# 52 of 72 attention probability tiles are turned in 32x32 blocks by VectorE, and their value products run in 32x64 tiles of TensorE

## The chip, the cores and the metric

One core of a Trainium2 chip runs the whole kernel in one launch. The metric is the device time of that launch in microseconds (us), the median of several runs.

## The reference

Two layers on 4 sequences of 1024 tokens with 256 channels, all in float32. The first layer (a linear attention with a running sum, then a mixture of 16 experts) and the last part (a mixture of 8 experts with a gate) are not touched. The change is in the attention of the second layer:

```
q, k, v = (rows of the normalized x) @ Wq, Wk, Wv      # 16 heads of 64 columns
q, k = apply_rope(q), apply_rope(k)                     # t * cos + rotate_half(t) * sin
sim = (q * 64 ** -0.5) @ k.T, masked above the diagonal
out = softmax(sim) @ v                                  # per head, 1024 x 64
y = concat(out) @ Wo
```

The two heads of a pair are computed together, so there are 8 pairs for each of 4 sequences.

## The kernel before, in words

The function `attention` is called twice: once for three sequences ("at", with the routing of the following mixture of experts beside it) and, after the mixture of experts, once for the last sequence ("at2", with the gating of the finished sequences on GpSimd). Each call runs 8 pairs a sequence, one turn of the loop a pair. What each engine does in a turn, and in which order, is written out in strings: `PE_ORDER`, `ACT_ORDER`, `DVE_ORDER` (lines 1192 to 1197) for TensorE, ScalarE and VectorE. A word is a kind of step with its numbers; a plus sign means that the step belongs to the next pair, so that two pairs overlap. `PE_FIRST`, `ACT_FIRST` and `DVE_FIRST` are the fill. The steps, with t the block of 128 query rows (0 to 7), k the block of 128 key rows and e the head of the pair:

- **A** (TensorE, lines 1550 and 1556): projections. For each half of 512 tokens, A0/A4 is q, A1/A5 is k (two products of 512 columns each), A2, A3, A6, A7 are v, 256 tokens each. ScalarE copies q and k to `raw` (line 1634), VectorE copies v (line 1843).
- **swap** (SyncE's queue, line 1383): four copies within SBUF exchange the halves of each head into `swapped`. **P** (VectorE, line 1850): raw x cos and swapped x sin. **rotate** (GpSimd, line 1656) adds the two into `qkT`.
- **S** (TensorE, line 1565): scores of row block t, chunk c of up to 512 keys. The two heads lie in rows 0 to 63 and 64 to 127 of the array. **M** (VectorE, line 1830) adds the mask, writes the piece to `p` and keeps the row's negated maximum. **E** (ScalarE, line 1621) is the exponential in place, with the row sum.
- **T** (TensorE, line 1573): the probability tiles of 128x128, 36 a head, 72 a pair, are transposed into PSUM, up to four a bank, and ScalarE copies them to `pT` (line 1628, 20 copies a turn).
- **V** (TensorE, line 1587): values times `pT`, for 256 queries at a time (V0 to V3); the two heads use columns 0 to 63 and 64 to 127 of the array. ScalarE copies the result to `oT` (line 1640). **W** (TensorE, line 1597) is the output product; VectorE adds it, divided by the row sum, to `y` (line 1865; the reciprocals are **I**, line 1837).

The eight banks of PSUM are used in a ring, in the order of TensorE's string: the step that uses a bank again waits until it is read (`free`, line 1507). `p` has eight buffers (`LAG`), two per row block. On SyncE's queue stand the loads of the next weights, the swaps and, in "at2", the loads and stores of the gating (`pair`, line 1385). GpSimd adds in "at" the rows that it scatters to the experts (`send`), and in "at2" `begin`, `plus` and `finish` of the gating (lines 1673 to 1692); the tanh of the gating is ScalarE's, in front of the step named by `CLOSE_TANH`.

## Time and profile before

| | |
|---|---|
| median of 3 runs | 2525.26 us (2525.19 to 2533.8) |
| the profiled execution | 2526.91 us |
| its span, first to last instruction | 2525.0 us |
| mean granted clock of TensorE | 0.985 of full speed |
| a turn of the pair loop, in both stages | 39.35 us |
| the "at2" stage | 2182 to 2525 us of the span, 8 turns |

A busy share is the part of the span in which the engine works on something; TensorE's weight loads are listed apart from its matmuls and overlap them. A float32 matmul shows as two records, a transpose as one, and a matmul's record is longer than the distance to the next, because consecutive ones overlap in the array. So steps are read from start to start.

### The profile page before, as it was taken

To read this page: it belongs to the slowest core of one execution; us is meant where nothing else is said; L and a number is where in the kernel's file an instruction comes from. 1 tells how busy PE (TensorE), PEld (TensorE's weight loads), DVE (VectorE), ACT (ScalarE), POOL (GpSimd) and SP (SyncE) were. 2 spreads that over 40 slices of the span, in tenths; PEclk is the share of its full clock that TensorE was granted. 3 is DMA by queue.
4 is the path that set the end of the run, shared out by engine and by line. 5 is a ranking of instruction groups with operands and counts; after the bars stand their busy time and mean duration, and the time that the engine had idled before them with its cause. 6 is when DMAs were issued, how large, how long until landed. Compare 5 with 4: busy or idle time off the path is not lost. (4 is left out here: it accounts for less than half of the span.)

```text
span 2525.0 us, 45013 instructions
## 1 busy us (share of the span) xinstructions
PE 2423.9 (96%) x14680; PEld 1710.0 (68%) x14681; DVE 1316.0 (52%) x3690; ACT 1105.4 (44%) x2581; POOL 606.9 (24%) x535
## 2 busy tenths in 40 slices
PE   7999999999986999999999999998999999799997
PEld 5555555666665566666666666666899999566665
DVE  6766242222246766666666666665333333366665
ACT  3211111111124566666666666666222222276665
POOL 4002002444454233332111111110111111224341
PEclk9999999999989999999999999999999999899999
DMA  6013104965456132332111222122777676324331
GB/s 214 17 50 117 50 17 135 268 210 156 109 146 212 51 99 78 109 100 68 40 35 42 58 68 57 44 58 78 253 239 241 236 244 233 109 76 126 90 96 59
DMA packets 133964, 296.04 MB, mean 117 GB/s; under 512 B 16865, under 2 KB 87025, under 8 KB 123473
## 3 DMA queue, kind: packets, MB, share of 16 engines
q1 hardware_dynamic: 112896, 251.59, 31.4%
q0 software_dynamic: 20944, 42.94, 6.6%
q8 instruction: 60, 0.98, 0.2%
q14 instruction: 64, 0.52, 0.1%
HBM read 193.80 MB, written 67.12 MB: 103 GB/s over the span
## 5 line engine op out<-in xcount | busy, mean ns | idle before, releaser
L1621 ACT ACTIVATE at_p<-at_p,at_nmax 128x640 f32<-128x640 f32 (+7 forms) x512 | 392.5, 767 | 185.9 <-DVE at_nmax L1830 184.3
L1656 POOL TENSOR_TENSOR kept_big<-kept_xg 128x1024 f32<-128x1024 f32 x64 | 151.0, 2359 | 896.3 <-DVE kept_xg L1850 896.3
L1628 ACT ACTIVATE at_pT<-at_ps 128x512 f32<-128x512 f32 (+1 forms) x640 | 311.3, 573 | 106.6 <-PE at_ps L1573 106.6
L1830 DVE CUSTOM_DVE_ANT_0 at_p<-at_ps,atk_mask 128x512 f32<-128x512 f32 (+3 forms) x512 | 281.9, 585 | 141.9 <-PE at_ps L1565 141.2
L1573 PEld LDWEIGHTS at_ps<-kept_ident,at_p 128*128 128x128 f32 x2304 | 257.9, 142 | 111.3 <-issue 60.3
L1573 PE MATMUL at_ps<-kept_ident,at_p 128*128 128x128 f32 x2304 | 304.8, 278 | 11.5 <-ACT at_p L1621 10.8
L1565 PE MATMUL at_ps<-kept_big 64*128 64x512 f32 (+3 forms) x1536 | 299.9, 509 | 15.3 <-POOL kept_big L1656 12.5
L1587 PE MATMUL at_ps<-at_pT,at_v 128*64 128x256 f32 (+1 forms) x2560 | 270.2, 362 | 2.5 <-issue 2.5
L1865 DVE SCALAR_TENSOR_TENSOR kept_big<-at_ps,at_inv,kept_big 128x256 f32<-128x256 f32 x512 | 214.2, 476 | 88.2 <-issue 67.1
L1587 PEld LDWEIGHTS at_ps<-at_pT,at_v 128*64 128x64 f32 x2560 | 174.0, 137 | 115.7 <-issue 29.0
L1550 PE MATMUL at_ps<-atk_h,atk_w 128*128 128x512 f32 x512 | 239.9, 603 | 12.5 <-SPq L1364 12.5
L1065 PE MATMUL ex_ps<-kept_big 128*128 128x512 f32 x480 | 210.2, 597 | 0.9 <-ACT kept_big L1122 0.9
L1969 PEld LDWEIGHTS moe_ps<-moe_xT,moe_w 128*128 128x128 f32 x1696 | 197.6, 192 | 3.6 <-ACT moe_xT L2002 0.9
L1969 PE MATMUL moe_ps<-moe_xT,moe_w 128*128 128x128 f32 x1696 | 198.0, 275 | 0.7 <-ACT moe_xT L2002 0.7
L1565 PEld LDWEIGHTS at_ps<-kept_big 64*128 64x128 f32 x1536 | 129.2, 190 | 88.8 <-issue 53.5
L1065 PEld LDWEIGHTS ex_ps<-kept_big 128*128 128x128 f32 x480 | 91.9, 192 | 110.4 <-issue 109.7
L1127 ACT ACTIVATE kept_big<-ex_ps 128x512 f32<-128x512 f32 x64 | 38.2, 597 | 290.4 <-PE ex_ps L1065 268.3
L1947 POOL DMA_INDIRECT z_rows<-late_yo,late_to x71 | 68.8, 969 | 371.9 <-DVE late_yo L2030 371.9
L1550 PEld LDWEIGHTS at_ps<-atk_h,atk_w 128*128 128x128 f32 x512 | 92.0, 195 | 93.2 <-issue 80.0
L1830 DVE CUSTOM_DVE_ANT_0 at_p<-at_ps,atk_mask,at_nmax 128x128 f32<-128x128 f32 (+3 forms) x256 | 135.1, 546 | 27.6 <-PE at_ps L1565 27.3
L1850 DVE TENSOR_TENSOR kept_xg<-kept_xg,atk_cos 128x1024 f32<-128x1024 f32 x64 | 78.1, 1221 | 136.5 <-DMA kept_xg<-kept_xg 136.5
L1151 DVE TENSOR_TENSOR kept_big<-kept_big,ex_ps 128x512 f32<-128x512 f32 x64 | 44.0, 688 | 186.4 <-ACT kept_big L1127 186.4
(244 smaller groups left out, 3416.0 us busy)
## 6 DMA issues: line engine op xcount, KB each, us to landing
moe_w<-in_w_w SPq DMA_DIRECT2D x53, 1028.0 KB, 4.8
kept_xg<-kept_xg SPq DMA_DIRECT2D x256, 128.0 KB, 2.3
atk_first_w<-in_w_w SPq DMA_DIRECT2D x18, 1028.0 KB, 4.8
atk_w<-in_w_qkv SPq DMA_DIRECT2D x32, 384.0 KB, 3.1
slot_in<-kept_big SPq DMA_DIRECT2D x9, 1032.0 KB, 9.5
kept_big<-in_w_eg SPq DMA_DIRECT2D x16, 512.0 KB, 3.6
kept_big<-in_w_eu SPq DMA_DIRECT2D x16, 512.0 KB, 5.0
kept_big<-in_w_ed SPq DMA_DIRECT2D x16, 512.0 KB, 6.7
```

The costliest lines, as they stand in the source:

```text
L1065: last = pe.matmul(bank, w[:, k * F0 + f * P:k * F0 + (f + 1) * P], xT[u][k][:, :], start=k == 0, stop=k == KC - 1)
L1550: last = pe.matmul(banks[0], w[x][:, k * QKV + m * P:k * QKV + (m + 1) * P], h[:, k * T + half * CH:k * T + (half + 1) * CH], start=k == 0 ...
L1565: pe.matmul(banks[e][:, 0:to - at], qkT[x][e * DH:(e + 1) * DH, n * P:(n + 1) * P], qkT[x][e * DH:(e + 1) * DH, T + at:T + to], start=True ...
L1573: last = pe.transpose(banks[0][:, (i - 4 * j) * P:(i - 4 * j + 1) * P], p[(2 * t + e) % LAG][:, k * P:(k + 1) * P], ident[:, :])
L1587: last = pe.matmul(banks[0][e * DH:(e + 1) * DH, skip:QW], v[x][:, (k * 2 + e) * DH:(k * 2 + e + 1) * DH], pT[n][:, at + skip:at + QW], st ...
L1621: act.activation(buf, buf, ACT.Exp, bias=nmax[:, unit:unit + 1], scale=-1.0, accum_out=rsum[:, unit:unit + 1]).then_inc(exp_done, 1)
L1628: act.activation(dst, ring[RING_BANK[part][ev]][:, 0:(i1 - i0) * P].rearrange("p (k c) -> p k c", c=P), ACT.Copy).then_inc(t_read, 1)
L1656: pool.tensor_tensor(out=qkT[x][:, :].rearrange("p (m t) -> p m t", m=2)[:, :, half * CH:(half + 1) * CH], in0=raw[half][:, :].rearrange(" ...
L1830: ins = dve.tensor_tensor_reduce(out=p[unit % LAG][:, at:to], in0=ring[RING_BANK[part]["S", ((t, c), e), ahead]][:, 0:to - at], in1=mask[: ...
L1850: dve.tensor_tensor(out=both, in0=both, in1=table[:, half * CH:(half + 1) * CH].unsqueeze(1).to_broadcast([P, 2, CH]), op=ALU.mult).then_i ...
L1865: dve.scalar_tensor_tensor(out=part_y, in0=bank[:, t * C:(t + 1) * C], scalar=inv[:, unit:unit + 1], in1=part_y, op0=ALU.mult, op1=ALU.add ...
L1969: last = pe.matmul(bank[:, m * P:(m + 1) * P], w1[q][:, at:at + P], xT[u][:, k * P:(k + 1) * P], start=k == 0, stop=k == KC - 1)
```

## The change

It does the following:

- The tiles of keys 0 to 511 (`HALF` = 4 key blocks, 26 of 36 tiles a head) are no longer transposed by TensorE. VectorE's new step **X** turns them with one instruction per row block and head, which transposes each 32x32 block in its place, into `pB` (16 instructions a turn, of up to four tiles). The rows of a 128-row tile are then not keys in order: block (b, a) of a tile stands where rows of group a hold keys of group b of 32.
- The value product of these tiles is done for each 32-row group a of the array by itself, with the values of key group b in those rows; group a's result goes to its own PSUM bank. That is 4 (k) x 4 (b) x 2 (e) x 4 (a) = 128 matmuls of 32 rows by 64 columns, with (8 - k) x 32 moving columns. For it the values of keys 0 to 511 are replicated by 16 copies of 64 KB within SBUF a pair (`replicate`, on SyncE's queue), so that each row group has the values of each key group (`v_blocks`).
- The 20 tiles of keys 512 to 1023 are still transposed by TensorE, in six steps, and multiplied with 128 rows, into the same banks (32 matmuls of 128 to 32 columns).
- There is now one V a turn, for all 1024 queries, behind all X and all T of the pair; W0 stands behind all four copies of V (`O0` to `O3`).
- Values are projected 512 tokens at a time (A2, A6) and copied by ScalarE instead of VectorE. The rotation's two products go from VectorE to GpSimd, which does cosine, sine and addition (for pair 0 VectorE still does the sine product).
- The mask shrinks from 1024 to 640 columns. The orders, the fill and the waits are new: VectorE's turn now holds all M and X of the next pair, and the block transposes X4 to X7 stand at its end.

```diff
+PE_ORDER = ("A0+ A1+ A2+ S5.1 S6.0 S6.1 S7.0 S7.1 T4.0 T5.0 A4+ A5+ T6.0 T6.1 A6+ T7.0 T7.1 S0.0+ S1.0+ S2.0+ S3.0+ V0 S4.0+ S4.1+ W0 W1 "
+            "W2 S5.0+ W3")
+ACT_ORDER = ("E4.0 A0+ A1+ E4.1 A2+ E5.0 E5.1 E6.0 E6.1 T4.0 E7.0 A4+ A5+ E7.1 T5.0 T6.0 T6.1 A6+ T7.0 T7.1 E0.0+ E0.1+ E1.0+ O0 E1.1+ "
+             "E2.0+ O1 E2.1+ O2 O3 E3.0+ E3.1+")
+DVE_ORDER = ("M0.0.0+ M0.0.1+ I3 M1.0.0+ M1.0.1+ M2.0.0+ X0.0+ M2.0.1+ X0.1+ M3.0.0+ X1.0+ M3.0.1+ X1.1+ X2.0+ M4.0.0+ M4.0.1+ M4.1.0+ "
+             "M4.1.1+ W0.0 W0.1 W1.0 I0+ M5.0.0+ W1.1 I1+ W2.0 X2.1+ W2.1 W3.0 M5.0.1+ W3.1 X3.0+ M5.1.0+ M5.1.1+ M6.0.0+ M6.0.1+ M6.1.0+ "
+             "X3.1+ M6.1.1+ M7.0.0+ M7.0.1+ M7.1.0+ M7.1.1+ X4.0+ X4.1+ I2+ X5.0+ X5.1+ X6.0+ X6.1+ X7.0+ X7.1+")
+CLOSE_TANH = ("T", (7, 1), 0)
...
+                def replicate(of):
+
+                    sp.wait_ge(blocks_read, of + ONE)
+                    for b in range(QB):
+                        for a in range(QB):
+                            sp.dma_start(v_blocks[a * QR:(a + 1) * QR, b * HALF * P:(b + 1) * HALF * P],
+                                         v_top[b * QR:(b + 1) * QR, :]).then_inc(blocks_in, 16)
...
                     for half in range(2):
                         swap(it + 1, half)
                         half_free(half)
+                    sp.wait_ge(v_read, it * 2 + 4 + ONE)
                     if load_w is not None:
-                        sp.wait_ge(a_ps, it * 8 + 16 + ONE)
                         sp.dma_start(w[1 - u][:, :], load_w).then_inc(w_in[1 - u], 16)
+                    ready()
+                    replicate(it + 1)
...
                         elif kind == "V":
-                            pe.wait_ge(t_read, (of + 1) * TURNS + turned_before(2 * n + 2) + ONE)
-                            pe.wait_ge(v_read, of * 4 + n + 1 + ONE)
-                            for k in range(2 * (n + 1)):
-                                skip = max(0, k * P - n * QW)
-                                for e in range(2):
-                                    at = (k * 2 + e) * QW
-                                    last = pe.matmul(banks[0][e * DH:(e + 1) * DH, skip:QW], v[x][:, (k * 2 + e) * DH:(k * 2 + e + 1) * DH],
-                                                     pT[n][:, at + skip:at + QW], start=k == 0, stop=k == 2 * (n + 1) - 1)
-                            last.then_inc(o_ps, 1)
+                            pe.wait_ge(blocks_in, of * BLOCKS + BLOCKS + ONE)
+                            pe.wait_ge(turned, of * UNITS + UNITS + ONE)
+                            for k in range(HALF):
+                                for b in range(QB):
+                                    for e in range(2):
+                                        for a in range(QB):
+                                            rows, at = slice(a * QR, (a + 1) * QR), (b * HALF + k) * P + e * DH
+                                            keys = pB[e][rows, k * (TURN_STEP + P):k * TURN_STEP + TB * P].rearrange("p (t b c) -> p b t c", b=QB, c=QR)
+                                            last = pe.matmul(banks[a][e * DH:(e + 1) * DH, k * QR:TB * QR], v_blocks[rows, at:at + DH], keys[:, b],
+                                                             start=k == 0 and b == 0, stop=False)
+                            last.then_inc(blocks_read, 1)
+                            pe.wait_ge(v_read, of * 2 + 2 + ONE)
+                            pe.wait_ge(t_read, of * len(TURNS) + len(TURNS) + ONE)
+                            for a in range(QB):
+                                for k in range(HALF):
+                                    for e in range(2):
+                                        at = e * LOW_COLS + k * LOW_STEP
+                                        keys = pT[:, at + k * P:at + HALF * P].rearrange("p (t a c) -> p a t c", a=QB, c=QR)
+                                        last = pe.matmul(banks[a][e * DH:(e + 1) * DH, (HALF + k) * QR:TB * QR],
+                                                         v[x][:, k * P + e * DH:k * P + (e + 1) * DH], keys[:, a], start=False, stop=k == HALF - 1)
+                                last.then_inc(o_ps, 1)
...
+                    pool.wait_ge(qk_read, of * 4 + 2 * half + 2 + ONE)
...
+                    pool.tensor_tensor(out=out, in0=plain, in1=cos_of, op=ALU.mult).then_inc(cosed, 1)
+                    if of > 0:
+                        pool.wait_ge(swap_in[half], of * 64 + 64 + ONE)
+                        pool.tensor_tensor(out=other, in0=other, in1=sin_of, op=ALU.mult).then_inc(sined, 1)
+                    pool.wait_ge(cosed, of * 2 + half + 1 + ONE)
+                    pool.wait_ge(sined, of * 2 + half + 1 + ONE)
+                    pool.tensor_tensor(out=out, in0=out, in1=other, op=ALU.add).then_inc(rot_done, 1)
...
+                        elif kind == "X":
+                            t, e = n
+                            unit, keys = 2 * t + e, min(t + 1, HALF)
+                            dve.wait_ge(exp_done, of * UNITS + unit + 1 + ONE)
+                            dve.wait_ge(blocks_read, of + ONE)
+                            dve.transpose(strided(pB[e][:, t * P:(t + 1) * P], TURN_STEP, keys), tiles(p[unit % LAG][:, 0:keys * P], keys)).then_inc(turned, 1)
```

## Rows read from the trace of the kernel before

**Rows 1.** The page's busy time of each engine: us, share of the span, instructions.
```profile
PE 2423.9 (96%) x14680; PEld 1710.0 (68%) x14681; DVE 1316.0 (52%) x3690; ACT 1105.4 (44%) x2581; POOL 606.9 (24%) x535
```
**Rows 2.** Stretches: a turn of "at", one of "at2"; busy us (instructions), PEclk, DMA share, GB/s.
```profile
1251.35:1290.70 39.35, 39.35 (x282) 26.76 (x280) 25.29 (x76) 25.38 (x60) 4.71 (x2) 1.00 0.17 40
...
2283.44:2322.79 39.35, 39.35 (x282) 26.78 (x281) 25.29 (x77) 26.32 (x61) 15.15 (x8) 1.00 0.37 107
```
**Rows 3.** TensorE in order of time, one turn of "at2": start, us, line, operation, count.
```profile
2322.63 3.60 PE L1550 MATMUL at_ps<-atk_h,atk_w 128*128 128x512 f32 x8
2326.06 1.05 PE L1556 MATMUL at_ps<-atk_w,atk_h 128*128 128x128 f32 x8
...
2330.72 2.38 PE L1587 MATMUL at_ps<-at_pT,at_v 128*64 128x256 f32 x24
2333.03 0.70 PE L1565 MATMUL at_ps<-kept_big 64*128 64x256 f32 x4
...
2346.28 2.60 PE L1587 MATMUL at_ps<-at_pT,at_v 128*64 128x256 f32 x24
2348.81 3.06 PE L1573 MATMUL at_ps<-kept_ident,at_p 128*128 128x128 f32 x26
2351.70 1.95 PE L1556 MATMUL at_ps<-atk_w,atk_h 128*128 128x128 f32 x16
...
2354.44 3.46 PE L1587 MATMUL at_ps<-at_pT,at_v 128*64 128x256 f32 x32
2357.83 2.00 PE L1597 MATMUL at_ps<-atk_wo,at_oT 64*128 64x256 f32 x16
```
**Rows 4.** TensorE's weight loads in order of time, 2330.6 to 2330.9 us.
```profile
2330.71 0.20 PEld L1587 LDWEIGHTS at_ps<-at_pT,at_v 128*64 128x64 f32 x4 [0.76 <-ACT at_pT L1628]
```
**Rows 5.** Groups by line and shape, whole kernel: count, busy us, mean ns, idle before.
```profile
L1628 ACT ACTIVATE at_pT<-at_ps 128x512 f32<-128x512 f32 x512 | 281.9, 617 | 14.8 <-PE at_ps L1573 14.8
...
L1587 PEld LDWEIGHTS at_ps<-at_pT,at_v 128*64 128x64 f32 x2560 | 174.0, 137 | 115.7 <-issue 29.0 <-ACT at_pT L1628 13.6
...
L1656 POOL TENSOR_TENSOR kept_big<-kept_xg 128x1024 f32<-128x1024 f32 x64 | 151.0, 2359 | 896.3 <-DVE kept_xg L1850 896.3
...
L1850 DVE TENSOR_TENSOR kept_xg<-kept_xg,atk_cos 128x1024 f32<-128x1024 f32 x64 | 78.1, 1221 | 136.5 <-DMA kept_xg<-kept_xg 136.5
...
L1634 ACT ACTIVATE kept_xg<-at_ps 128x512 f32<-128x512 f32 x128 | 75.2, 587 | 60.1 <-PE at_ps L1550 59.9
...
L1621 ACT ACTIVATE at_p<-at_p,at_nmax 128x1024 f32<-128x1024 f32 x64 | 72.8, 1138 | 0.4 <-DVE at_nmax L1830 0.4
...
L1843 DVE COPY at_v<-at_ps 128x256 f32<-128x256 f32 x128 | 53.1, 416 | 79.4 <-PE at_ps L1556 78.7
...
L1614 ACT ACTIVATE kept_big<-kept_big 128x1024 f32<-128x1024 f32 x8 | 8.7, 1089 | 0.0
```
**Rows 6.** VectorE in order of time, 2322.7 to 2362.2 us.
```profile
2330.53 0.69 DVE L1830 CUSTOM_DVE_ANT_0 at_p<-at_ps,atk_mask 128x512 f32<-128x512 f32 x1
2331.14 0.08 DVE L1830 DVE_READ_ACCUMULATOR2_ANT at_nmax<- 128x1 f32 x1
2331.14 0.35 DVE L1830 CUSTOM_DVE_ANT_0 at_p<-at_ps,atk_mask,at_nmax 128x128 f32<-128x128 f32 x1
...
2331.42 0.35 DVE L1830 CUSTOM_DVE_ANT_0 at_p<-at_ps,atk_mask,at_nmax 128x128 f32<-128x128 f32 x1
...
2359.07 3.23 DVE L1865 SCALAR_TENSOR_TENSOR kept_big<-at_ps,at_inv,kept_big 128x256 f32<-128x256 f32 x8 [2.00 <-issue]
```
**Rows 7.** The swap's transfers (issues, KB, us to landing); two issues on SyncE's queue.
```profile
kept_xg<-kept_xg SPq DMA_DIRECT2D x256, 128.0 KB, 2.3
...
2360.25 0.91 SPq L1439 DMA_DIRECT2D kept_big<-z_rows  x2
```
**Rows 8.** TensorE in order of time, the end of the span (2525.0 us).
```profile
2510.12 3.46 PE L1587 MATMUL at_ps<-at_pT,at_v 128*64 128x256 f32 x32 [1.25 <-issue]
2513.51 2.00 PE L1597 MATMUL at_ps<-atk_wo,at_oT 64*128 64x256 f32 x16
```

233 lines of the change are left out of this document (126 added, 107 removed).

## The prediction

> **What bounds the kernel now.** I read the page's busy table first: TensorE is busy for 96% of the span, VectorE for 52%, ScalarE 44%, GpSimd 24% [rows 1]. A whole-kernel share can hide a stage with another limit, so next came the table of stretches, two turns of the pair loop, one from each attention stage [rows 2]: a turn takes 39.35 us in both, TensorE is busy for all of it at full granted clock, VectorE for 25.3 us, ScalarE for 25.4 to 26.3, GpSimd for 4.7 and 15.2. There are 32 such turns, about half of the kernel; the rest is untouched by the diff. So a turn costs what TensorE's queue costs, and the order of time on TensorE [rows 3] says what that is. From the start of one group to the start of the next: 26 transposes take 2.89 us, 0.111 us each; the value products take 2.31, 2.53 and 3.39 us in a turn, 8.2 in all; a 512-column projection record takes 0.43 us (3.43 for eight), that is 0.84 ns a column.
>
> **What the change takes from TensorE.** 52 of 72 transposes go: 52 x 0.111 = 5.8 us. The old value products go: 8.2 us. Projections, scores and the output product keep their columns. What is left is 39.35 - 5.8 - 8.2 = 25.35 us a turn, plus the new value product, V.
>
> **What V costs.** This is the term that decides. A float32 product is two records a matmul. The lower part (keys 0 to 511) is 128 matmuls of 32 rows by 64 columns, 256 records; one of the eight tiles has, for k = 0 to 3, four times (8 - k) x 32 columns, twice: 4 x 832 x 2 = 6656 columns, at 0.84 ns 5.6 us. If all eight tiles run side by side that is the whole price. Two tiles do run side by side today: the 32 value records of mostly 256 columns take 3.39 us, 0.106 each, where one of 256 columns alone would be 0.215 [rows 3]. If never more than two do, the lower part costs 4 x 5.6 = 22.4 us. These are the two ends for the width. The upper part (keys 512 to 1023) is 64 records of 128 to 32 columns in pairs of tiles, 2560 columns x 0.84 = 2.15 us at least, and 64 x 0.111/2 = 3.6 at a transpose's step for each pair; I take 2.7. The other question is the feed: 320 matmul and 320 weight-load records must come in V. After a wait, four loads of 137 ns stood within 0.20 us [rows 4], so three starts in 0.063 us, 21 ns apart: 640 x 0.021 = 13.4 us if that were the sustained step; but matmul and load of one product start together, so it is a ceiling on a short burst, not a measured rate. The densest long stretch (2.31 us for 24 pairs, 0.096 each) would give 320 x 0.096 = 30.7 us, but that stretch is full of columns, so it shows a pace that the array set. I take eight tiles side by side, since both kinds of neighbour (two column tiles here, two row tiles in the scores) overlap fully and nothing in the rows shows a limit at two: V = 5.6 + 2.7 + 0.7 for the changes of tile shape and the stagger = 9.0 us. The ends 8 and 31 go into the range.
>
> The Trainium skill, "TensorE: Matmul & The Clock Gate", section "Step-by-step: what each phase is for", says that the sequencer needs about 62 ns for each MATMUL when it decodes in software. No stretch of this trace is dense enough to show or refute it over more than a few records. An estimate by that page would be 320 x 62 = 19.8 us for V against my 9.0, and with the other terms below a time of about 2738 against my 2415. A feed that binds is the first rival; its price there comes from rows.
>
> A turn on TensorE: 25.35 + 9.0 = 34.4 us.
>
> **VectorE.** It loses four rotation products of 1221 ns and four value copies of 416 ns, 6.5 us [rows 5]. It gains 16 block transposes over 6656 columns. No such operation is in the trace. The nearest row is the masked score piece: 512 columns take 0.61 us from start to start, 128 take 0.28 [rows 6]; by these and the line between them 10 of 0.61, 2 of 0.50, 2 of 0.38 and 2 of 0.28 make 8.4 us. An SBUF operand is no slower than the PSUM one of that row; below I put 7, above twice, 16.8, should a transposing pass fill and then empty. I take 8.4: VectorE goes to 27.2 us a turn.
>
> What matters more than its sum is a loop in the new orders. V waits for the last block transpose (X7.1); the fourth row of scores (S4.0+) stands behind V on TensorE; and VectorE's whole second half stands behind that. From V's end: 1.05 us to the first piece of S4, then 16 score pieces of 8.4 us, 16 additions of the output product at 3.23/8 = 0.40 [rows 6], 6.4 us, 11 block transposes, 6.6 us, three reciprocals, 0.5: 23.0 us to X7.1. The loop by VectorE is 23.0 + V = 32.0, 2.4 us under TensorE's 34.4.
>
> **ScalarE.** 14 of the 20 transposed-tile copies go, about 7.3 us; two 512-column value copies (587 ns) come; the four output copies stay four of 256 columns: some 19.5 us a turn. But its order crosses the loop: E7.1, T5.0, T6.0, T6.1, A6+, T7.0, T7.1 are in series behind M7.1.1, and S3.0+ needs the banks of T7.0 and T7.1. Counted from V's end: M5.1.0 ends at 12.3; E5.0 to E6.1, T4.0 and E7.0 follow and wait twice for VectorE, to 18.7; A4+ and A5+ to 19.9; E7.1 1.24, to 21.1; three copies 1.5; A6+ 0.6; T7.0 and T7.1 1.2, to 24.4 (durations in [rows 5]); then S3.0+ on TensorE 0.85: 25.4 with the signals, a loop of 34.4 with V. No slack against TensorE's sum. Two chains of equal length never fit perfectly; I add 0.8 us. A turn: 35.2 us. In the last sequence the tanh stands in front of the copy of T7.1; 1.09 us long [rows 5], of which I charge 0.5 us a turn.
>
> **GpSimd.** A rotation becomes three passes of 2359 ns instead of one [rows 5]: 14.2 us a turn, 24.7 with the gating of the last sequence. Cover: raw half 0 is copied some 9.7 us behind V's end; cosine pass and swap run together (four issues at 0.45 us, landing 2.3 us [rows 7]), then 2 x 2.36: ready at 18.5, and S0.0+ asks for it at about 21.8. The cover is 3 us; a late rotation would cost its lateness in each turn. The passes could be slower than 2.36 beside a busy VectorE; every one in the trace, beside rotation products too, is 2.36.
>
> **DMA queue.** 16 SBUF copies of 64 KB a pair: 16 x 0.45 = 7.2 us of issue, behind V's lower part and ahead of the next wo load and swap, which is asked for 9.7 us behind V's end. They fit; nobody waits for them until the next V, a turn later. The next w load is issued later, behind A6+'s copy, and used a turn later still.
>
> **The ends.** The fill is as long as before: the first rotation still waits for landing, one VectorE and one GpSimd pass. The drain is longer. Before, 11.5 us of span follow the last value product, for two of four output groups [rows 8]; now four groups follow, and V stands alone after X7.1. Against the seven turns before it I get 4 us more for the second attention stage and 6 for the first.
>
> **Sum.** 39.35 - 35.2 = 4.15 us a turn, for 30 turns (7 and 23 between the two fills and drains): 124.5; less 10 for the ends and 4 for the tanh: 110. The profiled execution took 2526.9 us for its span of 2525.0; 2526.9 - 110 = 2417. It lies 1.65 over the median of 2525.26, so I predict 2415.
>
> **The rivals.**
> 1. *TensorE can't be fed, or runs fewer tiles at once* (slower). Place: the lower part of V. Everything in the loop waits for V, so it adds one to one. It decides from V = 13.2: there 25.35 + 0.8 + 13.2 = 39.35. With four tiles at a time the lower part is 11.2, V 14.6, a turn 40.75: 1.4 x 30 + 14 = 56 slower, 2581. With the feed the limit, V by rows is between 13.4 and 30.7; at the middle, 22, a turn is 48.2: 8.8 x 30 + 14 = 278, 2803. For: 640 records in a few us, where now 80 pairs take 8.2. Against: pairs of tiles start together today.
> 2. *VectorE becomes the bound* because a block transpose costs twice a pass: 11 of them in the loop add 6.6, 29.6 + 9.0 = 38.6, and with 0.8 39.4: 2540, about the same or a little slower with the ends. For: no row shows one. Against: every one-input or masked pass here runs at about 1.05 ns a column.
> 3. *GpSimd's rotation is late*, by 3 us more than reckoned: +2 us a turn, 2415 + 60 = 2475. Still faster.
> 4. The change does all it says and the two loops fit without loss, V at 8.3: 33.7 a turn, 2370.
>
> **How the numbers follow.** Forecast 0.50, rival 1 0.28 (half of it each), rival 2 0.07, rival 3 0.08, rival 4 0.07. About 12 us (0.5%) is what a measurement can tell from no change. Faster: 0.50 + 0.08 + 0.07 = 0.65, less 0.02 for a forecast that slips to the edge, 0.63; same: that 0.02 and 0.03 of rival 2, 0.05; slower: rival 1 and the rest of rival 2, 0.32. The forecast's own range is 2375 to 2470. The range has to take in four tiles at once (2581) and a feed that binds mildly (V = 17 makes 43.2 a turn, 2656), and leaves out the far half of rival 1 and little below rival 4: 2365 to 2680.
>
> **What would show it.** Right: V's 256 records within about 6 us, stretches with six to eight tiles open; turns of about 35 us with TensorE busy nearly throughout. Wrong: records of V at an even step of 40 to 90 ns whatever their columns (feed), or four abreast; VectorE's transposes of 512 columns over 0.7 us; TensorE idle in front of S0.0+ until GpSimd's addition. A turn under 33 us would say that I counted a cover twice.

## The result and the profile after

The changed kernel took 2576.47 us (median of 4 runs, 2568.72 to 2583.39), the kernel before 2527.35 beside it: 1.019 times as long, 95% interval 1.0173 to 1.0207. Forecast was 2415. The profiled execution is one of 2574.89 us, with a span of 2573.1.

The page of the kernel after: busy time of each engine (compare [rows 1]), and two of its DMA queues. The last line is the same queue on the page of the kernel before.

```profile
PE 2333.7 (91%) x20696; PEld 1656.8 (64%) x20697; DVE 1393.5 (54%) x3950; ACT 925.6 (36%) x2197; POOL 900.4 (35%) x659
...
q0 software_dynamic: 20944, 42.94, 6.6%
q8 instruction: 156, 2.56, 0.4%
```
```profile
q8 instruction: 60, 0.98, 0.2%
```

TensorE was given less to do (2424 us busy before, 2334 after) and still ends later: it now stands idle for 239 us of the span, where it was 101. The second thing to see is queue q8, by which instructions come from memory in packets of 16 KB (its kind on the page is "instruction"): 156 of them instead of 60.

The answer to [rows 2], from the start of one blocks product V to the start of the next: one turn among the first eight of "at", two successive turns in the middle of it, one of "at2" (columns: stretch, us, busy us and instructions of PE, PEld, DVE, ACT, POOL, granted clock, DMA share, GB/s).

```profile
1005.82:1054.62 48.80, 41.12 (x468) 27.93 (x469) 27.34 (x85) 20.18 (x49) 23.29 (x17) 0.90 0.35 97
1309.11:1342.93 33.82, 33.82 (x469) 24.15 (x469) 27.29 (x85) 19.49 (x49) 13.85 (x7) 1.00 0.31 75
1342.93:1379.86 36.93, 33.99 (x469) 24.08 (x469) 27.29 (x85) 19.50 (x49) 14.22 (x7) 1.00 0.30 75
2377.43:2422.79 45.36, 39.04 (x470) 25.55 (x468) 27.50 (x84) 20.57 (x49) 24.50 (x12) 0.88 0.40 118
```

So there are four kinds of turn, not one. A clean one takes 33.8 us against 39.35 before, less than the 35.2 forecast. But in the loops of the middle only every second turn is clean; the others take 36.9 to 40.3 us. The turns of the first sequence take 42 to 49 us and those of "at2", but for the last, 40 to 45. In the two shown the mean granted clock is 0.90 and 0.88: TensorE pauses there and is then granted 1.2 GHz for a while (0.50 of full speed from 1014.9 to 1020.9 us), so that the clock adds to the price of the pauses.

Inside a clean turn the product is what the forecast said. TensorE in order of time (start, us, line, operation, count), and VectorE's block transposes of another such turn:

```profile
1309.11 6.06 PE L1627 MATMUL at_ps<-at_pB,at_v_blocks 32*64 32x256 f32 x256 [0.35 <-DVE at_nmax L1895]
1315.10 2.66 PE L1637 MATMUL at_ps<-at_pT,at_v 128*64 128x128 f32 x64
1317.69 0.70 PE L1606 MATMUL at_ps<-kept_big 64*128 64x512 f32 x2
```
```profile
1337.52 3.65 DVE L1912 STREAM_TRANSPOSE at_pB<-at_p 128x512 f32<-128x512 f32 x6
```

V takes 8.6 us (1309.11 to 1317.69), 9.0 forecast, and its lower part 6.0, where four tiles at a time would need 11.2: eight tiles do run side by side. A block transpose of 512 columns takes 0.61 us, as forecast.

**Loss 1: the head of every second turn.** TensorE, 1353 to 1361 us:

```profile
1356.60 1.14 PE L1646 MATMUL at_ps<-atk_wo,at_oT 64*128 64x256 f32 x8
1360.52 0.69 PE L1591 MATMUL at_ps<-atk_h,atk_w 128*128 128x512 f32 x1 [2.79 <-DVE kept_big L1931]
```

The view puts the 2.79 us down to VectorE's addition at L1931, which had been done long before. Nothing that the profile shows was awaited. What is special about the place is that TensorE's loop jumps back here, once in two turns (its branch instruction stands at 1356.7), and that packets of q8 came in at 1357.7 and 1360.8. The loops of the two stages jump back eight times in all, and behind each of these jumps TensorE stands still for 2.7 to 3.6 us.

**Loss 2: a product that starves, in the first eight turns.** TensorE, and GpSimd's `send` issues (L1729) in the same stretch:

```profile
1012.11 0.52 PE L1627 MATMUL at_ps<-at_pB,at_v_blocks 32*64 32x160 f32 x6 [0.21 <-issue]
1012.84 0.52 PE L1627 MATMUL at_ps<-at_pB,at_v_blocks 32*64 32x160 f32 x6 [0.21 <-issue]
```
```profile
1008.32 2.36 POOL L1724 TENSOR_TENSOR kept_big<-kept_big,kept_xg 128x1024 f32<-128x1024 f32 x1
1010.82 1.01 POOL L1729 DMA_INDIRECT slot_in<-kept_big,kept_tok_slot  x1
```

Five or six matmuls, then 0.21 us of nothing, "issue" (no wait for data), every 0.73 us: 12 instructions in 0.73 us where the clean product takes 12 in 0.14. From its first record to its last the lower part takes 8.8 us in this turn and up to 12.7 in others; in the clean turn it is 5.8.

The larger wait of these turns stands ahead of V. TensorE's waits in the first seven of them (us in total, times, longest), and VectorE a turn later:

```profile
PE at_ps L1627 <- DVE at_nmax L1895: 18.2, 7, 3.0
PE at_ps L1627 <- issue: 7.6, 27, 0.9
```
```profile
1051.02 0.29 DVE L1895 CUSTOM_DVE_ANT_0 at_p<-at_ps,atk_mask 128x128 f32<-128x128 f32 x1 [1.45 <-PE at_ps L1606]
1053.16 0.29 DVE L1895 CUSTOM_DVE_ANT_0 at_p<-at_ps,atk_mask 128x128 f32<-128x128 f32 x1 [1.85 <-PE at_ps L1606]
```

V needs the banks that VectorE's masks (M) read, and the first two masks start 1.45 and 1.85 us late, though TensorE had begun their scores at 1048.8. GpSimd's first group of four transfers is issued from 1046.95 to 1051.81 us. The whole list has no wait for GpSimd's rotation.

**Loss 3: scores that wait for the rotation, in "at2".** SyncE's queue, then GpSimd, then TensorE:

```profile
2384.97 11.59 SPq L1415 DMA_DIRECT2D at_v_blocks<-atk_first_w  x16
2396.60 1.59 SPq L1485 DMA_DIRECT2D out<-kept_big  x1
2398.24 0.43 SPq L1421 DMA_DIRECT2D atk_wo<-in_w_wo  x1
2400.79 0.81 SPq L1477 DMA_DIRECT2D kept_big<-z_rows  x2
2401.64 0.44 SPq L1478 DMA_DIRECT2D kept_big<-x_rows  x1
2402.12 0.43 SPq L1480 DMA_DIRECT2D kept_big<-y_rows  x1
2402.60 11.92 SPq L1408 DMA_DIRECT2D kept_xg<-kept_xg  x8
```
```profile
2411.98 2.39 POOL L1721 TENSOR_TENSOR kept_xg<-kept_xg,atk_sin 128x1024 f32<-128x1024 f32 x1 [7.44 <-DMA kept_xg<-kept_xg]
```
```profile
2371.64 2.93 PE L1606 MATMUL at_ps<-kept_big 64*128 64x128 f32 x12 [6.44 <-POOL kept_big L1724]
...
2417.00 2.68 PE L1606 MATMUL at_ps<-kept_big 64*128 64x128 f32 x12 [2.35 <-POOL kept_big L1724]
```

The swap goes out behind four gating loads and lands some 7 us after its issues; GpSimd's sine pass waits 7.44 us for it and the scores wait for GpSimd, 30.7 us in the seven intervals of "at2". The issue itself is hardly late: the cosine pass, which waits for the same copy of ScalarE as the swap, starts at 2402.17, and the swap is issued at 2402.60. It is the landing that takes long, while the DMA engines are 88 to 106% busy (2402 to 2410 us).

### The profile page after: what moved, and what is told of

The parts are those of the page before. It is cut to its first block and busy times, and to the rows that moved or that the text cites. A ratio compares the mean times of both kernels' runs of the same rounds, so it can differ in the third digit from the quotient of the medians.

```text
span 2573.1 us, 57872 instructions
## 1 busy us (share of the span) xinstructions
PE 2333.7 (91%) x20696; PEld 1656.8 (64%) x20697; DVE 1393.5 (54%) x3950; ACT 925.6 (36%) x2197; POOL 900.4 (35%) x659
## 5 line engine op out<-in xcount | busy, mean ns | idle before, releaser
L1912 DVE STREAM_TRANSPOSE at_pB<-at_p 128x512 f32<-128x512 f32 (+3 forms) x512 | 283.4, 588 | 249.0 <-PE at_ps L1627 214.0
L1606 PE MATMUL at_ps<-kept_big 64*128 64x512 f32 (+3 forms) x1536 | 312.0, 538 | 81.7 <-POOL kept_big L1724 53.3
L1718 POOL TENSOR_TENSOR kept_big<-kept_xg,atk_cos 128x1024 f32<-128x1024 f32 x64 | 151.5, 2368 | 449.5 <-ACT kept_xg L1693 449.3
L1627 PE MATMUL at_ps<-at_pB,at_v_blocks 32*64 32x256 f32 (+1 forms) x8192 | 233.9, 360 | 34.2 <-DVE at_nmax L1895 18.9
L1606 PEld LDWEIGHTS at_ps<-kept_big 64*128 64x128 f32 x1536 | 144.2, 201 | 178.5 <-issue 93.0
L1627 PEld LDWEIGHTS at_ps<-at_pB,at_v_blocks 32*64 32x64 f32 x8192 | 193.7, 140 | 93.5 <-issue 70.0
L1931 DVE SCALAR_TENSOR_TENSOR kept_big<-at_ps,at_inv,kept_big 128x256 f32<-128x256 f32 x512 | 213.2, 474 | 25.3 <-PE at_ps L1646 25.1
L1721 POOL TENSOR_TENSOR kept_xg<-kept_xg,atk_sin 128x1024 f32<-128x1024 f32 x60 | 141.8, 2363 | 143.2 <-DMA kept_xg<-kept_xg 143.2
L1724 POOL TENSOR_TENSOR kept_big<-kept_big,kept_xg 128x1024 f32<-128x1024 f32 x64 | 151.3, 2364 | 23.6 <-DVE kept_xg L1916 15.0
L1693 ACT ACTIVATE kept_xg<-at_ps 128x512 f32<-128x512 f32 x128 | 72.6, 590 | 223.2 <-PE at_ps L1591 223.2
L1699 ACT ACTIVATE at_oT<-at_ps 128x256 f32<-128x256 f32 x128 | 45.6, 377 | 289.2 <-PE at_ps L1637 289.0
```

Of the source, the lines that this page charges most:

```text
L1606: pe.matmul(banks[e][:, 0:to - at], qkT[x][e * DH:(e + 1) * DH, n * P:(n + 1) * P], qkT[x][e * DH:(e + 1) * DH, T + at:T + to], start=True ...
L1627: last = pe.matmul(banks[a][e * DH:(e + 1) * DH, k * QR:TB * QR], v_blocks[rows, at:at + DH], keys[:, b], start=k == 0 and b == 0, stop=False)
L1718: pool.tensor_tensor(out=out, in0=plain, in1=cos_of, op=ALU.mult).then_inc(cosed, 1)
L1721: pool.tensor_tensor(out=other, in0=other, in1=sin_of, op=ALU.mult).then_inc(sined, 1)
L1724: pool.tensor_tensor(out=out, in0=out, in1=other, op=ALU.add).then_inc(rot_done, 1)
L1912: dve.transpose(strided(pB[e][:, t * P:(t + 1) * P], TURN_STEP, keys), tiles(p[unit % LAG][:, 0:keys * P], keys)).then_inc(turned, 1)
```

## The experiments

The measure used throughout: V's starts. In the kernel after the first, 8th and 24th product of "at" and the first and last of "at2" start here, so the first seven intervals sum to 321.2 us, the next sixteen to 582.5, the seven of "at2" to 294.6:

```profile
872.18 1.12 PE L1627 MATMUL at_ps<-at_pB,at_v_blocks 32*64 32x256 f32 x32 [3.04 <-DVE at_nmax L1895]
...
1193.41 1.16 PE L1627 MATMUL at_ps<-at_pB,at_v_blocks 32*64 32x256 f32 x16
...
1775.94 0.73 PE L1627 MATMUL at_ps<-at_pB,at_v_blocks 32*64 32x256 f32 x8 [2.47 <-DVE at_pB L1912]
...
2249.25 0.47 PE L1627 MATMUL at_ps<-at_pB,at_v_blocks 32*64 32x256 f32 x8
...
2543.82 0.73 PE L1627 MATMUL at_ps<-at_pB,at_v_blocks 32*64 32x256 f32 x8 [2.02 <-ACT at_pT L1679]
```

All variants are edits of the changed kernel but b1; the row "before" is 7, 16 and 7 times the 39.35 us of [rows 2]. A star: part of the product is left out.

```
                          us    ratio to before     first 7  next 16  "at2" 7  q8 packets
before                  2527.4                       275.5    629.6    275.5      60
after                   2576.5  1.0173 to 1.0207     321.2    582.5    294.6     156
f0_after (again)        2581.5  1.0196 to 1.0242     316.6    577.9    294.8     156
e1_straight             2502.5  0.9865 to 0.9920     265.1    566.1    293.8     141
e2_send_late            2532.5  1.0002 to 1.0033     275.4    581.1    298.2     156
e3_rot_dve              2576.8  1.0174 to 1.0220     276.3    616.3    298.7     156
e4_swap_first           2487.2  0.9816 to 0.9848     275.2    583.8    249.1     156
f1_spread               2598.2  1.0255 to 1.0292     287.9    633.9    295.0     158
f2_straight_swap        2501.3  0.9875 to 0.9908     313.1    570.1    245.3     141
f3_v_half*              2428.7  0.9581 to 0.9632     278.8    510.1    268.5      66
g1_late4_swap           2471.7  0.9754 to 0.9814     252.8    589.5    248.9     156
g2_late4_straight_swap  2437.3  0.9627 to 0.9659     243.6    569.0    245.6     141
g3_direct               2532.0  1.0005 to 1.0043     275.2    581.9    294.9     156
b1_straight             2525.5  0.9981 to 1.0001                                  95
h1_half_spread*         2366.7  0.9335 to 0.9376     217.2    509.5    267.9      66
h2_late4_rot_dve        2501.9  0.9875 to 0.9908     259.2    600.1    258.2     141
h3_v_three*             2452.8  0.9684 to 0.9717     256.4    535.2    274.1     101
h4_half_mid*            2408.8  one run              239.6    530.2    267.5      66
h5_mid                  2530.9  one run              257.5    587.4    298.7     156
```

### The loop body

e1_straight: TensorE alone runs its turns without `Fori`.

```
         def run(eng, act_on, straight=False):
             act_on("first", -1, -1, 1, -1)
+            if straight:
+                for at in range(nb * PAIRS - 1):
+                    act_on("both", at, at % PAIRS, at % 2, at // PAIRS)
+                act_on("last", nb * PAIRS - 1, PAIRS - 1, 1, nb - 1)
+                return
```

> TensorE's head-pair turns are written out one after another, with no backward branch; every other engine and every instruction stays. Theory A (the loop): the loop body of two turns has 1,994 instructions of TensorE where the body before had 1,284, and after the jump at the end of the body its instructions have to be fetched again, so that TensorE stands still for 2.8 to 5.0 us at the head of every second turn. Then all these gaps go: 14 or 15 of them at some 3 us, about 45 us, with what the half clock after them costs perhaps 60: 2515 to 2535 us. Rival (the wait is a real one, for the PSUM or projection buffer that the profile names, or for the VectorE): the gaps stay, 2576 us. Rival that the feed is too slow in itself (any stretch of 64-column instructions): the gaps move into the blocks product V, which grows beyond 6 us in all turns, and the time stays or rises, 2570 to 2650 us.

It gained 74 us, more than expected. 16 of them lie in the middle stretch, as much as its five pauses behind a jump (16.4 us); its long turns are gone (mostly 33.9 to 35.5 us now, with a 40 at each new sequence). 56 lie in the first seven turns, more than their stalls; of those below. In "at2" the stalls' time went to the next wait, for the swap. b1_straight does the same to the kernel before:

> Control: the kernel before with TensorE's turns in one line. Its loop body of 1,284 instructions was fetched 60 times in all and never within the loops of the second and third sequence; now it is fetched as it goes, about 115 times. TensorE is busy without a gap there, and its wide matmuls leave a fetch more time than the 64-column blocks do: 2527 us, no change within 0.3%. If fetching as such costs, 2550 us or more.

No change, 95 fetches: fetching as such cost nothing in that kernel, whose matmuls are mostly wide. f3_v_half shortens the body instead, `for b in range(QB // 2)` in V's lower part:

> Left out is half of the lower blocks product: the value blocks 2 and 3 of the four (128 of its 256 matmuls a turn). TensorE's loop body has 1,482 instructions (95 KB) instead of 1,994 (128 KB). Directly that takes 3.0 us of TensorE's 6.0 a turn, 32 x 3 = 96 us: 2480 us if the number of instructions has no effect of its own. If the body now stays in the engine's instruction buffer, as the 1,284 instructions (82 KB) of the kernel before do, the stall at every second turn's head goes too and the products run clean: the fetches fall from 156 to about 60, and the time to 2370 to 2410 us. If 95 KB is still too much, some 120 fetches are left, and 2460 to 2480 us.

The fetches fell to 66, and the middle turns are all alike, 30.8 to 31.2 us but for one at each new sequence. Each turn is 3.1 us shorter by the matmuls left out (5.9 to 2.8 in V's lower part), sixteen make 50; the stretch fell by 72. Of the other 22 us the five pauses are 16.4. The time, 2429 us, is above the 2370 to 2410 expected, by the first seven turns. h3_v_three (`range(QB - 1)`) looks for the size:

> Left out is a quarter of the lower blocks product (value block 3 of four): TensorE's loop body has 1,738 instructions, 111 KB, between the 95 KB that stayed in the buffer and the 128 KB that did not. Directly it saves 1.5 us a turn, 48 us: 2530 us. If the body stays in the buffer, the fetches fall from 156 to 70 or so and the stall of every second turn goes besides: 2475 to 2500 us. If not, some 135 fetches and 2520 to 2540 us.

101 fetches, and here the loops differ. Of the eight passes that follow a jump back, three fetched the body again, 8 or 9 packets each (both in the first sequence, one of three in the second), and begin with a pause of 3.16, 3.03 and 3.20 us; the other five fetched one packet or none and begin without one. TensorE behind two of these jumps, a pass that is fetched and one that is not:

```profile
1283.21 1.12 PE L1591 MATMUL at_ps<-atk_h,atk_w 128*128 128x512 f32 x2 [3.20 <-DVE kept_big L1931]
...
1215.10 1.13 PE L1591 MATMUL at_ps<-atk_h,atk_w 128*128 128x512 f32 x2
```

So a body of 95 KB (f3) is kept in every loop, one of 111 KB in some passes, one of 128 KB in none: each of the eight passes in the changed kernel fetches 9 or 10 packets. What decides at 111 KB is open. The time is 22 to 47 us below what was expected, by the first seven turns. The sizes are 64 bytes for each instruction, 16 KB for 256 of them: in e1, where nothing is kept, 13,482 instructions in a row took 52 packets, 259 each. A turn has 468 matmuls and 468 loads where it had 280 of each; with 122 others (164 before) that is 1,994 for the two turns of the body instead of 1,284.

The Trainium skill, "Runtime: NRT & Kernel Launch", section "Instruction fetch mechanics", gives TensorE's instruction memory as 128 KiB, 2,048 instructions, refilled in blocks of 16 KiB, and says that a taken branch to a block outside the current window of two stalls the engine for a fetch. The packet size and the stall agree. The rest does not: 1,994 instructions are fewer than 2,048 and were fetched in each pass, and the kernel before, whose body fills five blocks, fetched nothing between 1214 and 1469 us, over six turns of its loop, which fits neither a window of two blocks nor the section's sentence that no instruction cache gains from code lying close together.

### The order of GpSimd's queue in the first sequence

In the changed kernel a turn's eight indirect transfers stand in two groups, one between the halves of the rotation and one behind them. e2_send_late puts `pool.wait_ge(o_ps, QB * of + ONE)` ahead of the second group:

> GpSimd's second group of four indirect transfers in each of the first eight turns (the first layer part's rows being sent out) waits until the blocks product V of the pair is done. Theory B: each such issue takes TensorE's feed of instructions away while GpSimd writes its descriptors, so that V goes on in bursts of six matmuls with a fifth of the time empty and then at half the clock, 8.8 to 12.7 us instead of 6.0 for its lower part. Then V is back to 6 us in all the turns but those where the first group falls on it, 3 to 6 us of each of the first seven turns, and 20 to 45 us in all: 2530 to 2555 us. Rival (the V of these turns is long because its operands, the transposed blocks or the value columns, come late there): V stays at 9 to 12 us and the time at 2576 us. It costs nothing on GpSimd unless its rotation passes come late behind the sends: then up to 5 us in each of seven turns, 2600 us.

The time fell by 44 us, but not as the theory says: V's lower part stayed at 8.7 to 9.9 us in six of the first seven turns. What is gone there is the wait for the masks and the bursts; in their place V stands still once, for some 2 to 2.7 us, of which more at g3_direct. f1_spread moves the transfers: four a turn over sixteen turns, behind both halves (SyncE's wait for the last of them moves along).

```
                         rotate(of, 0)
-                        j = of - 1
+                        rotate(of, 1)
+                        j, part = divmod(of - 1, 2)
 ...
-                            send(j, range(0, TB // 2))
-                        rotate(of, 1)
 ...
-                            send(j, range(TB // 2, TB))
+                            send(j, range(part * TB // 2, (part + 1) * TB // 2))
```

> GpSimd's 64 indirect transfers are spread over sixteen turns instead of eight, four a turn behind both of its rotation halves; the rest is the changed kernel. Theory B2 (TensorE's instructions come through the DMA engines, two or three fetches of 16 KB within each blocks product, and the traffic of eight indirect transfers of 128 rows delays these fetches by 2 us): with half the traffic a turn and none of it inside the first half of a turn, the blocks product of the first eight turns is back to 6 to 7 us; from 46 (or 39) us a turn to 35 to 37, and the next eight turns lose at most 1 us: 2500 to 2545 us, or 20 us below the changed kernel if that takes 2530 in this call. Rival (the product is long there for its own operands): no change.

A miss: 22 us slower. In eleven of the sixteen turns the issues now meet V's lower part, which takes 9.9 to 11.6 us in nine of them, in the same bursts, and 7.5 and 7.8 in two; in the other five it takes 5.6 to 5.8. TensorE, one product of f1_spread:

```profile
921.20 0.52 PE L1627 MATMUL at_ps<-at_pB,at_v_blocks 32*64 32x160 f32 x6 [0.21 <-issue]
```

g1_late4_swap adds the wait for the product ahead of everything that GpSimd does for the transfers (and the swap's order, below):

> Two changes to the changed kernel: the swap's first half ahead of the loads (last part: 249 us from the first to the last blocks product, measured), and the 64 indirect transfers spread over sixteen turns, four a turn, each group now behind both rotation halves and behind the blocks product (in the spread tried before they fell into it). If the first turns are slow because transfers fall on the product and on the score masks ahead of it (VectorE stands still for 1 to 3 us there), turns 1 to 15 take 35 to 38 us: from the first to the 24th product 840 to 870 us instead of 859 (the swap variant) or 904: 2455 to 2490 us. If any transfer costs TensorE its 1.3 us wherever it lies, nothing is gained against the swap variant: 2487 to 2500 us.

In the second to the sixteenth turn V's lower part is 5.6 to 6.3 us, and the 23 intervals take 842.3 us, 921.8 in f1_spread and 903.7 in the changed kernel. Are the transfers harmful, or only together with fetches? h1 and h4 take half of the product away, so that nothing is fetched in the loops, and place the transfers behind both halves (h1) and between the cosine and sine pass of half 1 (h4); h5 is h4 with the whole product.

> Left out is half of the lower blocks product, as before, so that TensorE's loop body of 1,482 instructions stays in its buffer; the indirect transfers are spread over sixteen turns with no wait for the product, so that they fall on its lower or upper part. If they slow TensorE only by delaying fetches of instructions, nothing of it is seen in the loops where no fetch is made: products of 2.8 and 2.7 us, and turns of 31 us. If GpSimd's writing of descriptors slows the delivery of instructions to TensorE in itself, the products run in bursts of six matmuls each 0.73 us as long as the four issues last, from about 1 us after the first: a product of 2.8 or 2.7 us takes 5 to 7, the turns 33 to 38 us, and the time is 2430 to 2450 us.

> Left out is half of the lower blocks product again (TensorE's loop body fits), and the four indirect transfers of a turn stand between the cosine and the sine pass of half 1, so that they are issued from some 2 us ahead of the product to its end. With no fetch of instructions in the loops: if the transfers slow the delivery of instructions in themselves, the products run in bursts (six matmuls each 0.73 us) and the lower one takes 5 us instead of 2.8; if they do so only where a fetch is under way, it stays at 2.8. In either case the rotation's half 1 is ready 5 us later, which costs a turn 2 to 3 us: 2400 to 2430 us.

> The same place of the transfers with the whole product (the loop body of 1,994 instructions, fetches within each product). Products that fall together with the four issues must show the bursts, 9 to 12 us instead of 6 for the lower one, in each of the first sixteen turns: 41 us or more a turn, 2590 to 2620 us.

h1 is clean, 30.8 us a turn from the second on. It is f3_v_half with the transfers behind the rotation's halves, four a turn, instead of between and behind them, and that alone is worth 62 us. It looks like the recorded rival of the late rotation, but f3's waits in its first seven turns say otherwise:

```profile
PE at_ps L1627 <- DVE at_nmax L1895: 19.0, 8, 3.1
...
PE at_ps L1606 <- POOL kept_big L1724: 0.6, 1, 0.6
```

TensorE waits 0.6 us for the rotation and 19.0 us ahead of V for VectorE's masks, as in loss 2; in h1 that wait is 3.0 us, ahead of the first V. h4 puts the transfers into half 1 of the rotation, and there it is late (14.2 us of waits for GpSimd's addition in the first seven turns). They also fall on the product, and this is what it looks like without a fetch, TensorE and then GpSimd:

```profile
1075.81 3.10 PE L1627 MATMUL at_ps<-at_pB,at_v_blocks 32*64 32x256 f32 x128
1078.84 2.66 PE L1637 MATMUL at_ps<-at_pT,at_v 128*64 128x128 f32 x64
```
```profile
1073.81 1.05 POOL L1730 DMA_INDIRECT slot_in<-kept_big,kept_tok_slot  x1
1075.16 0.97 POOL L1730 DMA_INDIRECT slot_in<-kept_big,kept_tok_slot  x1 [0.30 <-issue]
1076.43 0.97 POOL L1730 DMA_INDIRECT slot_in<-kept_big,kept_tok_slot  x1 [0.30 <-issue]
1077.71 0.97 POOL L1730 DMA_INDIRECT slot_in<-kept_big,kept_tok_slot  x1 [0.30 <-issue]
```

No bursts: the product is at full pace under four issues, with the DMA engines 104% busy (1076 to 1078 us), and so in all the products of h4's loops. The transfers hurt the product only where its instructions are fetched. h5 was a miss in the other direction (2531, not 2590 or more): its lower products take 6.1 to 9.6 us, not 9 to 12. In the one at 1059.9 us, of 6.4 us, the issues end at 1062.4 and the fetch starts at 1061.7, so they hardly meet. The longest, at 1021.91, has no bursts but one pause of 3.49 us, like those of the next run.

g3_direct replaces the eight indirect transfers by one plain one of the same bytes, between the halves of the rotation:

> The eight indirect transfers of a turn are replaced by one plain transfer of the same 1 MB to consecutive rows (rows then lie in other slots than the router says; the expert part computes on them all the same). Bytes and place stay; seven of GpSimd's eight issues of 1.28 us a turn go. If it is GpSimd's writing of the descriptors that holds up TensorE and VectorE (and the rotation behind it), the first seven intervals fall from 46 us to 35 to 37 each, by 65 to 75 us: 2505 to 2515 us. If it is the traffic, which delays TensorE's instruction fetches, they stay at 44 to 46 us and the time at 2576.

44 us less than the changed kernel, between the two expectations, and V's lower part stays at 8.5 to 10 us in the first seven turns, as in e2 and e4 which keep the eight issues. TensorE in one of these products, and the stretch of it (DMA share and GB/s last):

```profile
988.47 4.75 PE L1627 MATMUL at_ps<-at_pB,at_v_blocks 32*64 32x256 f32 x181
995.91 1.66 PE L1627 MATMUL at_ps<-at_pB,at_v_blocks 32*64 32x192 f32 x75 [2.69 <-issue]
```
```profile
990.00:992.00 2.00, 2.00 (x99) 2.00 (x85) 0.00 (x0) 0.00 (x0) 0.00 (x0) 1.00 1.02 370
992.00:994.00 2.00, 1.22 (x53) 0.88 (x38) 0.00 (x0) 0.00 (x0) 0.69 (x1) 1.00 0.97 370
```

So a product can starve in two ways. Here there are no bursts but one pause: the DMA engines are full from 986 to 994 us, and the packet of q8 starts 5.0 us behind V's start, where in the clean turn it starts 2.4 behind. The bytes alone, under one issue, are enough for this, and h4 shows that they do nothing to a product without a fetch. The bursts come only beside indirect issues; while they run the DMA engines are 24% busy (the changed kernel, 1011.8 to 1014.9 us), so they are not the same thing, and how they arise was not tried.

### The swap in the last sequence

e4_swap_first issues the swap's half 0 ahead of the loads.

```
-                    then()
                     for half in range(2):
                         swap(it + 1, half)
                         half_free(half)
+                        if half == 0:
+                            then()
```

> In the last eight turns SyncE issues the swap's first half ahead of the loads of the expert rows instead of behind them; nothing else changes. Rival D (the swap is late in SyncE's queue): the swap's first half goes out by four issues, about 2.5 to 4 us, earlier in those turns, and the waits of the scores for the rotation, 2.4 to 6.7 us, shrink by 2 to 3 us in seven turns: 2556 to 2565 us. If the rotation is late for GpSimd's own work alone, nothing moves: 2576 us. If the expert loads that are now later are what the last addition waits for, 2580 to 2590 us.

"at2" lost 45.5 us, 6.5 a turn and not 2 to 3, and TensorE's waits for the rotation are gone there: the swap had not so much been issued late, its packets had stood behind those of the loads (median landing 7.3 us behind them, 2.7 ahead). Ahead of them the sine pass starts 3 us after the swap's last issue instead of 7, e4's SyncE and GpSimd:

```profile
2297.90 2.44 SPq L1408 DMA_DIRECT2D kept_xg<-kept_xg  x4
2300.38 1.08 SPq L1478 DMA_DIRECT2D kept_big<-z_rows  x2
```
```profile
2303.42 2.38 POOL L1722 TENSOR_TENSOR kept_xg<-kept_xg,atk_sin 128x1024 f32<-128x1024 f32 x1 [3.10 <-DMA kept_xg<-kept_xg]
```

The rest of e4's 89 us lies in the first seven turns, which it doesn't touch. f0_after was to say whether that was chance:

> The changed kernel itself once more, as it is. In the first layer part all other variants so far took 38 to 39 us for each of the first seven turns, though two of them change nothing there; the profiled execution of the changed kernel took 45.9. If that is something of this program (where its instructions lie, say), it repeats: 2576 us, and 46 us a turn. If it was something of one chip or one execution, the kernel now takes 2530 us and 39 us a turn, and what moving the loads did for the last layer part is 45 us rather than 89.

It repeats, 316.6 us. There are two rhythms of these turns, near 39 and near 45 us, and small edits elsewhere decide between them; e3, g3 and e4 fell into the one, the changed kernel and f2 into the other. In the slow one GpSimd's first group falls on the masks ahead of V and the second on V (the lines of loss 2), in the other the first group just ahead of V. What chooses stays open. So a part of what e2, e3, g3 and e4 gain or lose in their first column says nothing of their edit.

> TensorE's turns in one line and the swap's first half ahead of the loads: the two changes that gained 74 and 89 us alone. If they act in different places (the first layer part, the last one) and part of the 89 us belongs to neither, the first part takes 831 us from the first to the last blocks product as with straight-line turns alone, and the last part 245 us: 2502 less 46 us, 2450 to 2460 us, which beats the kernel before by 70. If both took away the same thing, 2487.

The slow rhythm again, 313.1, and so 2501 us and not the 2450 to 2460 expected; the other two columns are as expected.

### The rotation's engine

e3_rot_dve gives both products back to VectorE, two calls more in its order (P1+, and a new step for half 0), with GpSimd's addition alone left; h2_late4_rot_dve does it to the fastest variant.

> Both products of the rotation (cosine and sine) are VectorE's again for every pair, GpSimd only adds them: four passes a turn of about 0.3 to 0.6 us each go to VectorE and four of 2.36 us leave GpSimd. Theory C (the recorded rival that the rotation on GpSimd comes late): scores of the last eight turns wait 2.4 to 6.7 us for it, and 2 to 3 us in the first turns; if GpSimd's passes are what makes it late, 7 times 4 us in the last turns and some 15 us in the first ones go, against 4 x 0.5 us more on VectorE that has some 6 us of waiting a turn: 2530 to 2550 us. Rival D (the swap of halves through DMA is what is late, behind other issues of SyncE): the wait only moves to VectorE, where it now also holds up the masks and transposes behind it: 2576 to 2620 us.

> The fastest variant so far (2437 us: straight-line turns, transfers spread and behind the product, swap ahead of the loads) with both products of the rotation on VectorE and only the addition on GpSimd. Recorded rival of a late rotation: with the other obstacles gone GpSimd's passes would now be what is late, and giving them back would gain 1 us or more a turn, 2405 us. The prediction's view (VectorE's four more passes stand in the line of masks and transposes, and GpSimd's are covered): it costs 2 to 2.5 us a turn as it did alone (36.3 against 34.0 us a clean turn), 2437 + 60 to 75 = 2497 to 2512 us, the gain of the transfers' shorter way included.

A clean turn of e3 takes 36.3 us instead of 34, and "at2" gained nothing: what was late there was the swap. In h2 it costs 65 us. So the two products are cheaper on GpSimd than on VectorE, also with the other obstacles gone.

### All three together

> The same with TensorE's turns in one line, without a backward branch. The stall of some 3 us at every second turn's head is gone besides: 835 less 16 to 30 us from the first to the 24th product: 2430 to 2470 us. Straight-line turns and the swap's order alone took 2501 us, with 313 us in the first seven intervals; if that is how the fetches of straight-line code fall together with the transfers, it must now be 245 to 260 us.

2437.3 us, 0.9643 of the kernel before (0.9627 to 0.9659) and 139 us below the changed kernel, of which 78, 14 and 49 us lie in the three columns. One turn in each stage of g2, in a stretch of 35 us:

```profile
905.00:940.00 35.00, 34.31 (x471) 24.37 (x472) 27.38 (x85) 19.79 (x51) 18.12 (x10) 1.00 0.35 93
1246.00:1281.00 35.00, 34.96 (x479) 25.10 (x480) 28.35 (x87) 20.10 (x51) 19.20 (x11) 1.00 0.37 96
2290.00:2325.00 35.00, 34.16 (x472) 23.86 (x468) 27.73 (x87) 20.45 (x49) 24.39 (x11) 1.00 0.49 151
```

## Why the prediction was wrong

- **What V costs, and the clean turn**: right. V 8.6 us (9.0), VectorE 27.3 a turn (27.2), a block transpose of 512 columns 0.61 (0.61), ScalarE 19.5 (19.5), the clean turn 33.8 to 34.5 (35.2). Rival 1's place, eight tiles abreast, did not decide. Its price, 2581, came close to the result by another mechanism. The estimate by the 62 ns for each matmul of the Trainium skill ("TensorE: Matmul & The Clock Gate", section "Step-by-step: what each phase is for") fell too: 256 matmuls and 256 loads pass in 6.0 us, 23 ns for each matmul (the section gives the figure for decoding in software, and no trace here tells how it was done). The 1.05 ns a column given against rival 2 is in no row ([rows 6] has 0.61 us for 512 columns, 1.19 each); nothing hung on it. The 2656 for V = 17 in its range is 2655 by its own terms.
- **"The other question is the feed" is the step that failed first.** It asked how fast instructions start, and not where they come from. The count stood in [rows 2]: 560 records of each kind in two turns, to which the change adds 376 of each. With 1,994 instructions the body is no longer kept from pass to pass. This cost the stall at every second head (e1, f3, h3), 16.4 us in the middle stretch, and made V depend on one to three fetches each time, which other traffic delays (g3, against h4).
- **"GpSimd ... ready at 18.5 ... the cover is 3 us" failed in the first eight turns.** The reckoning left out the eight indirect transfers in the same queue, 8 x 1.28 = 10.3 us a turn, because the turn of [rows 2] from which it was made has none. They cost 62 us by f3 against h1, two kernels with the same 66 fetches. But the wait that the step and rival 3 speak of, TensorE's for a late rotation, is 0.6 us there; what came in its place is VectorE's masks, which stand still beside the issues and hold V up, 19.0 us in f3 and 18.2 in the changed kernel, and the starving of V. Why VectorE stands still was not tried.
- **"DMA queue ... they fit" failed in "at2".** The 16 copies take 10.5 to 11.6 us of issue, 0.7 each, not 7.2 (what that costs no run separates); and the swap's packets stand behind those of the loads: 45.5 us (e4). Here the rotation is late indeed, though not by GpSimd's own passes: rival 3 had this as 2 us a turn; it was 6.5 in "at2".
- **"The ends": 10 us forecast.** In g2 the 23 and 7 intervals are shorter than before by 92 and 30 us, 122 in sum; its time is shorter by 90. So the ends cost 32 (21 in the first attention stage, 11 in the second), 22 more than the sum allowed. 2415 + 22 is 2437: with the three obstacles gone the forecast's turn holds (243.6 and 245.6 us for seven, 246 forecast), and what is left is the ends. That three losses and a good turn added up to a small slowdown is chance.

The second, third and fourth places of this list are where the forecast broke, the first two of them together for 78 us in the first sequence and 14 in the middle, the last for 49 in "at2" (g2 against the changed kernel). The third and fourth are one error: a queue was reckoned from a turn in the middle of a stage, and those of the first and the last eight turns were not written out.

## What to carry to other kernels

A change that trades few wide matmuls for many small ones is paid for in instructions: count those of the loop body on the engine. Here 1,482 (95 KB) were kept in every loop, 1,738 (111 KB) in some passes and 1,994 in none; where a body passes the first of these, write fewer turns in it or none in a loop. The sign in a profile is a growing instruction queue, and idle time at the loop's head that is put down to something long done. Keep DMA bursts, GpSimd's transfers and their loads, away from stretches where short matmuls are being fetched, and GpSimd's indirect issues away from passes of VectorE that TensorE waits for. And in a queue put the short transfer that the next step waits for ahead of the large loads, in each stage by itself.

## What the runs showed of the hardware

- 512 TensorE instructions (32x64 tiles, float32) in 6.0 us, 11.7 ns each, as long as they are there.
- In products that fetch, four indirect transfers of GpSimd cut this to 12 in 0.73 us, 61 ns each; in products that fetch nothing they cut nothing (h4). Not each product in which both met showed it, and why is open.
- With the DMA engines full (share 0.97 to 1.04, 986 to 994 us in g3_direct) a packet of instructions comes some 2.6 us later than in a clean turn, and the product stands still for 2.69 us.
- TensorE keeps a loop body from pass to pass up to a size: 1,482 instructions in all eight repeated passes, 1,738 in five, 1,994 in none. A pass that is fetched again begins with 2.7 to 3.6 us of idle time.
- In f3_v_half two score masks of VectorE stood still for 1.26 and 1.85 us in a stretch in which GpSimd issued four transfers (1020.95 to 1025.81 us), with nothing awaited that was not done, and in the changed kernel for 1.45 and 1.85. The cause was not tried.
- After a pause the granted clock fell in some turns and not in others: behind 2.71 us of idle time at 2396.07 the eight-record projection took 5.39 us instead of 3.6, while the turn with a pause of 2.79 us at 1360.52 has a mean clock of 1.00. The slow turns have two such pauses, one ahead of V and one at the head.
